# Value products of two head groups in every fourth slot instead of one in every second, in a fused edge-filter, attention and feed-forward kernel

## What is computed

```
h = edge_filter(gray(x))                      # 8 x 256 x 256
h = h + attention(layernorm(h))               # 16 heads of 16, 256 tokens
h = h + ffn(layernorm(h))                     # 256 -> 1024 -> 256, silu, quantised weights

def attention(x):
    q, k, v = x@Wq+bq, x@Wk+bk, x@Wv+bv       # q, k then through Wp, head by head
    scores = q @ k.T / sqrt(16)
    return softmax(scores) @ v
```

## Time and profile before

| | |
|---|---|
| median of 3 runs | 300.62 us (299.88 to 300.94) |
| the profiled execution | 303.49 us, of which the span of the trace is 301.8 |
| TensorE, VectorE, ScalarE, GpSimd busy | 94%, 69%, 57%, 45% of the span |
| attention stage, first K block to last A block | 95.2 to 206.2 us |
| mean granted TensorE clock | 0.983 |

### The profile page before, as it was taken

The page is one execution under the profiler, slowest core; times in us unless marked ns, Lnnn a source line. Parts: engine busy times, 40 slices in busy tenths (PEclk is TensorE's granted clock), DMA queues, the critical chain, the costliest instruction groups (busy, mean ns, idle before and its releaser), DMA issues.

```text
span 301.8 us, 6338 instructions
## 1 busy us (share of the span) xinstructions
PE 283.3 (94%) x2336; PEld 220.3 (73%) x2336; DVE 208.2 (69%) x415; ACT 173.2 (57%) x330; POOL 137.1 (45%) x268
## 2 busy tenths in 40 slices
PE   5999699879998998999999999999999999999996
PEld 5886468667877655666666666667898998899896
DVE  8789959568989884788889887635845733641423
ACT  2547867753433783668776777867354344435350
POOL 7375554411000148663769572156859389500000
PEclk9999799999999996899999999999999999999999
DMA  6977543889898933566473000000000200200202
GB/s 203 296 229 232 126 152 142 206 189 334 224 313 275 320 109 100 156 201 229 137 201 86 3 2 0 2 2 1 2 0 0 73 0 0 73 0 0 72 0 70
DMA packets 27310, 35.90 MB, mean 119 GB/s; under 512 B 5184, under 2 KB 16272, under 8 KB 27280
## 3 DMA queue, kind: packets, MB, share of 16 engines
q1 hardware_dynamic: 27184, 35.43, 39.3%
q10 hardware_dynamic: 96, 0.07, 0.1%
HBM read 24.42 MB, written 10.49 MB: 116 GB/s over the span
## 4 chain that ended last, share of the span: by engine, by line
PE 65%; DVE 7%; DMA 7%; POOL 6%; ACT 6%; issue 5%; SPq 3%; ACTq 1%; POOLq 0%; DVEq 0%
PE bank L1208 35%; PE bank L1337 8%; PE bank L1289 7%; PE bank L1312 4%; PE bank L1317 4%; DMA wscale<-in_L_ffn_fc_scales 3%; PE bank L1355 3%; DVE negmax L909 2%; DMA halo_x<-in_x 2%; DMA bv<-in_L_attn_bv 2%; PE bank L1226 2%; PE bank L1347 1%; POOL gray_l L591 1%; SPq L422 1%; PE bank L1363 1%
## 5 line engine op out<-in xcount | busy, mean ns | idle before, releaser
L909 DVE TENSOR_REDUCE negmax<-bank 128x2 f32<-128x512 f32 x128 | 82.1, 684 | 7.5 <-PE bank L1289 7.0
L1116 ACT ACTIVATE probs<-bank 128x512 f32<-128x512 f32 x128 | 66.3, 603 | 30.0 <-PE bank L1317 30.0
L963 DVE TENSOR_TENSOR y_l<-yf,y_h 128x512 fp32r<-128x512 f32 x32 | 24.1, 752 | 38.4 <-ACT yf L1142 38.3
L1139 ACT ACTIVATE y_h<-bank,b1col 128x512 fp32r<-128x512 f32 x32 | 22.0, 688 | 48.0 <-PE bank L1208 47.9
L1208 PE MATMUL bank<-w_h,y_h 128*128 128x256 f32 x128 | 36.9, 288 | 0.4 <-DVE osb L971 0.4
L1208 PE MATMUL bank<-w_l,y_h 128*128 128x256 f32 x128 | 36.2, 283 | 0.0
L1208 PE MATMUL bank<-w_h,y_l 128*128 128x256 f32 x128 | 36.2, 283 | 0.0
L1337 PE MATMUL bank<-probs,vals 128*32 128x256 f32 x512 | 35.1, 393 | 0.0
L1289 PE MATMUL bank<-ks,qs 48*128 48x256 f32 x256 | 32.6, 333 | 1.3 <-DVE negmax L909 0.7
L1289 PEld LDWEIGHTS bank<-ks,qs 48*128 48x128 f32 x256 | 19.9, 190 | 15.0 <-DVE negmax L909 5.8
L1312 PE MATMUL bank<-negrow,pick 48*128 48x512 f32 x128 | 26.8, 415 | 0.6 <-DVE pick L1010 0.6
(11 more groups left out here) (158 smaller groups left out, 598.7 us busy)
## 6 DMA issues: line engine op xcount, KB each, us to landing
xr<-in_x SPq DMA_DIRECT2D x8, 768.0 KB, 7.4
qs<-qk_parts SPq DMA_DIRECT2D x48, 128.0 KB, 3.1
ks<-qk_parts SPq DMA_DIRECT2D x48, 128.0 KB, 3.2
qk_parts<-qk_h SPq DMA_DIRECT2D x16, 256.0 KB, 3.1
qk_parts<-qk_l SPq DMA_DIRECT2D x16, 256.0 KB, 3.2
wraw<-in_L_ffn_fc_q SPq DMA_DIRECT2D x4, 512.0 KB, 4.9
wscale<-in_L_ffn_fc_scales SPq DMA_DIRECT2D x4, 512.0 KB, 6.9
out<-osb SPq DMA_DIRECT2D x16, 128.0 KB, 1.8
```

Source lines behind the costliest of these rows:

```text
L909: eng.tensor_reduce(negmax[:, b % 2, u, v], entry_bank(key)[:, :].rearrange("p (t k) -> p t k", t=NT), AX.X, ALU.max, negate=True).then_in ...
L963: eng.tensor_tensor(y_l[:, p % 2, f], yf[:, n % 2], y_h[:, p % 2, f].bitcast(fp32), ALU.subtract).then_inc(s_y, 1)
L1116: eng.activation(probs[:, n % PBUF], p2[n % 4][:, :], ACT.Exp).then_inc(s_exp, 1)
L1139: eng.activation(y_h[:, p % 2, f], src, ACT.Silu, bias=b1col[:, f:f + 1])
```

## The change

Value products are issued for two groups together, in the slots 5, 9, 13, ... 61, and for one group in the slots 63 and 65 as before. The second group has the upper half of bank 7, and ScalarE copies both halves at once. `probs` gets a twelfth place. The neg and out blocks move to the same slots, ahead of the A blocks. The Q block stands ahead of the K block only in every fourth slot, where it did in every second. GpSimd's first weight step moves from slot 6 to slot 10, and the second layer's weights are loaded in the slots 23 and 24.

```diff
-    PBUF = 11
+    PBUF = 12
...
+        def attend_at(s):
+
+            if s % 4 == 1 and 5 <= s < SLOTS:
+                return ((s - 5) // 2, (s - 5) // 2 + 1)
+            if s in (SLOTS - 1, SLOTS + 1):
+                return ((s - 3) // 2,)
+            return ()
...
             b, i = s // UNITS, s % UNITS
-            if i in (3, 7) and b + 1 < B:
-                return (b + 1, i // 4)
+            if i == 1 and b < B:
+                return (b, 1)
+            if i == 5 and b + 1 < B:
+                return (b + 1, 0)
...
-            b, i = s // UNITS - 1, s % UNITS
-            if b >= 0 and i in ((3, 5) if b < B - 1 else (3, 4)):
-                return (b, i // 4 if b == B - 1 else (i - 3) // 2)
+            b, i = s // UNITS, s % UNITS
+            if b >= B:
+                return {3: (B - 1, 0), 4: (B - 1, 1)}.get(i)
+            if b >= 1 and i == 5:
+                return (b - 1, 0)
+            if b >= 2 and i == 1:
+                return (b - 2, 1)
+            if s == SLOTS - 1:
+                return (B - 2, 1)
...
-            spare = [s for s in range(6, SLOTS - 8) if s % 8 in (0, 2, 3, 4, 6, 7)]
+            spare = [s for s in range(10, SLOTS - 8) if s % 8 in (0, 2, 3, 4, 6, 7)]
...
-                eng.wait_ge(s_av, G + 1)
+                eng.wait_ge(s_av, G + 2)
...
-                eng.activation(otr_of(G), av[:, 0:N], ACT.Copy).then_inc(s_ot, 1)
+                eng.activation(otr_of(G, 2), av[:], ACT.Copy).then_inc(s_ot, 2)
...
-                if s % 2 == 1 and 3 <= s < SLOTS - 1:
-                    copy_av((s - 3) // 2)
+                if s >= 1 and len(attend_at(s - 1)) == 2:
+                    copy_av(attend_at(s - 1)[0])
...
-                if s % 2 == 0 and s + AHEAD < SLOTS:
+
+                if s % 4 == 0 and s + AHEAD < SLOTS:
                     scores_by_query(s + AHEAD)
                 if s < SLOTS:
                     scores_by_key(s)
-                if s % 2 == 1 and s + AHEAD < SLOTS:
+                if s % 4 and s + AHEAD < SLOTS:
                     scores_by_query(s + AHEAD)
...
-                if s % 2 == 1 and 0 <= s - 3 < 2 * GROUPS:
-                    for t in range(NT):
-                        attend((s - 3) // 2, t)
                 if neg_after(s):
                     neg(*neg_after(s))
                 if out_after(s):
                     out_rows(*out_after(s))
+                for G in attend_at(s):
+                    for t in range(NT):
+                        attend(G, t)
```

More of the change, by code:

```diff
@@ L143, in vit_tower_kernel @@
     probs = at("probs", 43, [P, PBUF, NT * N], fp32)
-    otr_b = at("otr_b", 65, [P, 2, N], fp32)
+    otr_b = at("otr_b", 135, [P, 2, N], fp32)
     otr_a = at("otr_a", 139, [P, 4, N], fp32)
@@ L158, in vit_tower_kernel @@
     nt_l = at("nt_l", 107, [P, 2, KE, COLS], fp32r)
-    yf = at("yf", 57, [P, 2, COLS], fp32)
-    osb = at("osb", 61, [P, 2, COLS], fp32)
+    yf = at("yf", 59, [P, 2, COLS], fp32)
+    osb = at("osb", 63, [P, 2, COLS], fp32)
     y_h = at("y_h", 143, [P, 2, FT, COLS], fp32r)
@@ L167, in norms_of, with otr_of @@
         return (xt2_h, xt2_l) if p % 2 else (xt_h, xt_l)
-    def otr_of(G):
+    def otr_of(G, n=1):
         r = G % OBUF
-        return otr_a[:, r] if r < 4 else otr_b[:, r - 4]
+        return (otr_a[:, r:r + n] if r < 4 else otr_b[:, r - 4:r - 4 + n]).rearrange("p g n -> p (g n)")
     ctx = ExitStack()
@@ L308, in vit_tower_kernel @@
                    ("qkv", 3, 0): 6, ("qkv", 3, 1): 7, ("qkv", 3, 3): 8, ("qkv", 3, 4): 9}
-        NEG_AT = {("qkv", 2, 5): 0, ("qkv", 3, 4): 1}
+        NEG_AT = {("qkv", 2, 5): 0}
+        def attend_at(s):
[4 more added lines that the diff above has]
+            return ()
         def neg_after(s):
             b, i = s // UNITS, s % UNITS
-            if i in (3, 7) and b + 1 < B:
-                return (b + 1, i // 4)
+            if i == 1 and b < B:
+                return (b, 1)
+            if i == 5 and b + 1 < B:
+                return (b + 1, 0)
         def out_after(s):
-            b, i = s // UNITS - 1, s % UNITS
-            if b >= 0 and i in ((3, 5) if b < B - 1 else (3, 4)):
-                return (b, i // 4 if b == B - 1 else (i - 3) // 2)
+            b, i = s // UNITS, s % UNITS
[7 more added lines that the diff above has]
+                return (B - 2, 1)
         END = SLOTS + 5
@@ L517, in _ @@
                                 load_qk(p, m, i)
-                if s in (19, 20):
-                    if s == 19:
+                if s in (23, 24):
+                    if s == 23:
                         eng.wait_ge(s_w1f, 2)
                     eng.wait_ge(s_p2, s)
-                    load_ffn(1, 2 * s - 38)
-                    load_ffn(1, 2 * s - 37)
+                    load_ffn(1, 2 * s - 46)
+                    load_ffn(1, 2 * s - 45)
             for p in range(PAIRS):
@@ L924, in copy_av @@
                 eng.wait_ge(s_av, G + 1)
-                eng.tensor_copy(otr_of(G), av[:, 0:N]).then_inc(s_ot, 1)
+                c = N * (G % 2)
+                eng.tensor_copy(otr_of(G), av[:, c:c + N]).then_inc(s_ot, 1)
             def moments2(p, j):
@@ L1186, in _ @@
                         edge(p + 2, 1)
-            neg_rows(0, 1)
             for s in range(SLOTS):
@@ L1322, in attend @@
                 b, g = G // 4, G % 4
+                c = N * (G % 2)
                 if t == 0:
-                    s = 2 * G + 3
-                    if s >= SLOTS:
+                    if G == GROUPS - 1:
                         eng.wait_ge(s_exp, 4 * (G + 1))
@@ L1332, in attend @@
                             wait_read(eng, ("qkv", PAIRS - 1, i))
-                    else:
+                    elif G % 2 == 0 or G == GROUPS - 1:
                         eng.wait_ge(s_ot, G)
@@ L1336, in attend @@
                     h = 4 * g + j
-                    ins = eng.matmul(av[OROWS * j:OROWS * (j + 1), 0:N], vals[:, b, t, h * VW:h * VW + OROWS],
+                    ins = eng.matmul(av[OROWS * j:OROWS * (j + 1), c:c + N], vals[:, b, t, h * VW:h * VW + OROWS],
                                      probs[:, (4 * G + j) % PBUF, t * N:(t + 1) * N], start=t == 0, stop=t == NT - 1)
```

## The result

The changed kernel takes **338.3 us** (median of 4 runs, 337.3 to 341.8) against 300.5 before. The ratio is 1.128, with a 95% interval of 1.120 to 1.137. The forecast was slower, 317.7 us, with a range of 309 to 327. So the direction held and the size did not.

What follows compares the result with a forecast made beforehand. A ring of three banks between TensorE's Q blocks and VectorE's maxima was taken to set the pace. Stretch terms +1.0, -2.5, +9.1, +3.3, +3.1, +3.1 gave +17.1 on 300.6: 317.7 us, range 309 to 327.

Steps and rivals of the forecast that it cites:

- The cycle of four slots: Attention stage: four waits of 1.30 plus out block, two groups and K block make 8.15 us, against 6.62 before.
- the out block's wait of 0.6: After neg, the out block waits for the maximum of the Q block whose bank it needs; 0.6 us a cycle.
- the starving: VectorE, from the last Q block to the next: 1.9 us of work in 4.25 us, so it starves for two microseconds.
- The order's terms: Attention stage: the new order's losses summed over the stretches, leaving out the 4.55 us expected from removing the stall.
- The three stretches given as +9.1: Slots 16-24, 24-32 and 40-48: 16.3 us each against 13.3, 13.2 and 13.2, together +9.1 us.
- The stretch behind slot 56: Slots 56 to the last A block: two more bursts at 1.5 us each, +3.1 us.
- I take the whole 4.55 as gained: Slots 8 to 16: `split_max` ahead of the weight steps removes the GpSimd stall and its lower clock, gaining 4.55 us.
- rival 3: TensorE's waits also lower the clock: 4 to 12 spells at 2.5 us each, 328 to 348 us; chance 0.08.
- The forecast's own sign of being wrong: VectorE idle under 1 us per cycle, clock below 1.00 in several stretches, or TensorE waiting for ScalarE's exponentials.
- Rival 1: The out block does not wait for its bank: 0.6 us less in each of 12 cycles, 310.5 us; chance 0.10.
- Rival 2: The ring does not couple TensorE and VectorE: cycles of 6.0 us, 289 us in total; chance 0.07.
- Rival 4: The stall stays or moves because weight steps come in a bunch or transfers later: 322 us; chance 0.07.

Runs made afterwards that it cites:

- the filler between the Q blocks: Changed kernel plus six idle transposes of the identity on TensorE between the two adjoining Q blocks, from slot 8 on: 324.8 us (one run).
- The half maximum: VectorE's row maximum over only half the keys: 312.1 us in the changed kernel, 293.0 us in the order before with weight steps four slots later.
- the filler experiments: Changed kernel plus idle transposes between adjoining Q blocks and ahead of the out block: both 327.4 us, only the first 324.8, only the second 336.0.
- the moved Q block: Changed kernel with the Q block ahead of the K block in slots 2, 6, 10, ... instead of 0, 4, 8, ...: 330.1 us.
- the A blocks first and the clock held: Changed kernel with A blocks ahead of neg and out block and six idle transposes between adjoining Q blocks: 317.8 us.

## Why the forecast was right in kind and wrong in size

The attention stage is read from the start of the first K block to the start of the last A block's last matmul in each trace: 106.4 us in the unstalled trace of before, 144.5 after, 130.5 with the filler between the Q blocks. The filler itself costs 8.23 - 8.12 = 0.11 us in some 12 cycles, 1.3. That splits the loss:

```
loss of the order, at full clock     130.5 - 1.3 - 106.4 = 22.8 us
loss of the lower clock              144.5 - 130.5 + 1.3 = 15.3 us
sum                                                        38.1 us
measured in the median               338.3 - 300.5       = 37.8 us
```

The close agreement of the last two lines is partly luck, since the start of attention alone moves by 1.7 us from trace to trace. The clock's 15.3 us include 2.7 in the slots 0 to 8 (16.10 us against 13.35 with the filler, at 0.79 and 1.00). There the filler does not run yet, so it did not prevent those two falls; what it is shown to remove is the other 12.6.

- **The cycle of four slots** held: 8.15 forecast, 8.11 to 8.12 measured. So did its parts, 1.24 to 1.29 us between Q blocks, 1.29 to the out block, and the out block's wait of 0.6 was shown by putting the A blocks ahead of it (7.48). The half maximum showed that the release by the maximum sets these distances. VectorE's idle 35 us is the starving that the forecast described.
- **The order's terms**, without the stall's gain, came to 17.1 + 4.55 = 21.7 us; measured 22.8. (The three stretches given as +9.1 add up to 9.2.) Slots 0 to 16 were right to 0.4 us once the clock is set aside (13.35 and 15.56 us with the filler, for 13.0 and 15.3). The stretch behind slot 56 was forecast at +3.1 and is +3.9 with the filler (8.85 + 10.28 against 7.38 + 7.82 before); the waits there I had not worked through one by one.
- **The step "I take the whole 4.55 as gained" failed.** The stall was in one trace of two; the shift is worth 1.3 us in the old order and nothing that can be measured in the new. I had also seen that the median lay 2.9 us below the profiled execution and started from the median, yet took off a stall that only the profiled execution is known to have. Without it the forecast would have been 300.6 + 21.7 = 322.3, so this step is 3.3 to 4.6 us of the miss of 20.6.
- **The step that failed most is rival 3**, "in cycles the waits are 1 us at most", from which I gave the clock a chance of 0.08 and the sum no term. The clock fell eleven times in attention, once in most cycles, for 15.3 us, 1.4 a spell. The number in the rival was right (4 to 12 spells). Its price was not: 2.5 us came from a spell of 6.8 us (115.5 to 122.3 in the trace before), and those of the changed kernel last 3.4. Eleven at 2.5 would be 345 us, so that the measured 338 lies in the rival's 328 to 348 is in part luck. The chance was far off. I had read from the earlier trace rows that a wait of 2.0 us goes before a fall, and took it for the measure of what is needed. No row showed that waits of 1 us and less in each cycle would not do; the filler experiments show that they do, and the moved Q block shows that waits of 0.5 us can. The forecast's own sign of being wrong, a clock column below 1.00 in several stretches, came true. I had also named the two losses as alternatives when they add up.

On the falls the Trainium skill (TensorE: Matmul & The Clock Gate, A second HAM failure mode: psum-queue depth-cycling) is right: groups of matmuls that go round PSUM banks with short idles between make the clock swing. The traces agree, with waits of 0.25 to 0.78 us ahead of the matmuls of a cycle.

- **Rival 1** (the out block does not wait) is refuted by the 0.6 us that the A blocks ahead of it take off the cycle. **Rival 2** (faster, the ring doesn't couple them) is refuted by the maxima's timing. **Rival 4** (stall stays or moves) did not come: the stretch of slots 8 to 16 has no wait on GpSimd.

Three things stay open. Why the clock also falls at the start of the stage, in some executions and versions and not in others (at 96.9 us in the changed kernel, nowhere in the stage with one filler, which begins at slot 8), was not tried apart. Whether the falls follow the longest wait, the sum of the waits or something else is not shown. And what the pairing of the A blocks costs by itself, with the out block and the Q blocks where they were before, no run shows: with the A blocks first and the clock held, 317.8 us, some 17 us of loss are left.

## What to carry to other kernels

Where two engines hand a short ring of buffers back and forth, the distance of the producer's blocks matters more than their number: merging blocks to save a drain of 0.1 us opened a gap of 4.3 us between two Q blocks (at full clock) that a ring of three could not bridge. Price such a change as a loop (issue, result, release, next issue) before counting what it saves. And when a change makes TensorE wait regularly, add the clock as a term of the sum, not as a rival: here it was 40% of the loss, and useless transposes in the longest wait brought most of it back. Before a stall seen in one trace goes into a sum, look at a second trace.

## What the runs showed of the hardware that I had not expected

- The granted clock falls to 1.2 GHz for spells of 3.4 us in a stage where no matmul waits longer than 1.0 us and matmuls fill 6.60 of a cycle's 8.11 us. With the wait of 0.78 us between the adjoining Q blocks filled, or cut to 0.51 by the half maximum, it stays at 2.4 GHz behind slot 8; with the Q block moved it falls four times there though no wait in a cycle is over 0.5 us.
- At the lower clock the A blocks took 3.08 us for 1.9, while the cycle as a whole lost 1.1 to 1.6 us of its 8.1; I read this as the matmuls at the lower clock lying partly in what would be TensorE's waits for VectorE.
- The same kernel starts its attention stage at 95.2 or 96.9 us by how often the clock falls in the stage ahead, and in the two traces this goes with whether a transfer that lands at 109.2 to 109.7 us is late.
